# Macaron block: the weighted sums of attention steps 1 to 14 by pairs of heads, in two banks

## The reference

```
x = x + 0.5 * ffn(layernorm(x))
x = x + attn(layernorm(x))
x = x + 0.5 * ffn(layernorm(x))

ffn:  logits = x @ router_w + router_b; top 2 of 8 experts, softmax over the two
      combined = sum_e w_e * silu(x @ expert_w[e].T + expert_b[e])
      y = x + combined @ proj_w.T + proj_b;  rms norm, times norm_w
attn: 16 query heads, 4 key and value heads, head size 128, rope on q and k
      scores = q k^T / sqrt(128), causal;  softmax;  out = P v;  out @ wo.T
```

## Time and profile before

| | |
|---|---|
| median of 3 runs | 827.48 us (825.24 to 830.95) |
| profiled execution, its own time | 827.55 us |
| its span, first to last instruction | 825.8 us |
| TensorE matmul / weight load busy | 792.3 / 697.7 us |
| VectorE / ScalarE / GpSimd busy | 651.9 / 507.4 / 517.2 us |
| share of the chain that ended last | TensorE 82%, VectorE 6%, GpSimd 5%, ScalarE 3% |

### The profile page before, as it was taken

How to read it: one execution, slowest core, us unless ns; L and a number is a source line. 1 busy time by engine, 2 the same in 40 slices (tenths; PEclk the granted TensorE clock), 3 DMA queues, 4 the chain that set the end, 5 groups by cost and what they waited for, 6 DMA issues and landing times.

```text
span 825.8 us, 16045 instructions
## 1 busy us (share of the span) xinstructions
PE 792.3 (96%) x4712; PEld 697.7 (84%) x4712; DVE 651.9 (79%) x1917; ACT 507.4 (61%) x1250; POOL 517.2 (63%) x408
## 2 busy tenths in 40 slices
PE   7899999859999999999999999999999999999996
PEld 4688878658999999999899998999999988788885
DVE  6988996886677686786866868768687799988876
ACT  3565565567667586675765767557576586444543
POOL 4636648693878778787777777877878761112302
PEclk9999999978999999999999999999999999999998
DMA  9245412201132122212312313132131110000001
GB/s 295 86 135 191 148 58 52 52 13 39 27 77 73 41 51 76 51 25 64 102 26 50 88 30 85 27 88 51 31 96 25 39 27 1 1 1 26 2 26 52
DMA packets 28998, 50.09 MB, mean 61 GB/s; under 512 B 3874, under 2 KB 9634, under 8 KB 28962
## 3 DMA queue, kind: packets, MB, share of 16 engines
q1 hardware_dynamic: 28964, 49.67, 21.5%
HBM read 18.72 MB, written 9.96 MB: 35 GB/s over the span
## 4 chain that ended last, share of the span: by engine, by line
PE 82%; DVE 6%; POOL 5%; ACT 3%; issue 2%; DMA 1%; SPq 0%; POOLq 0%; DVEq 0%; ACTq 0%
PE pt L1696 8%; PE pj L1631 5%; PE pj L1633 5%; PE pj L1632 5%; PE o L1710 5%; PE o L1711 4%; PE o L1712 4%; PE sc L1685 4%; PE sc L1684 4%; PE sc L1683 4%; PE pj L1740 4%; PE pj L1742 3%; PE pj L1741 3%; PE sc L973 3%; PE sc L975 3%; PE sc L974 3%
## 5 line engine op out<-in xcount | busy, mean ns | idle before, releaser
L1260 POOL TENSOR_TENSOR at_ql<-at_rot,at_qh 128x512 fp32r<-128x512 f32 x64 | 82.7, 1292 | 103.0 <-ACT at_qh L1485 102.9
L1387 DVE TENSOR_TENSOR at_ptl<-pt,at_pth 128x512 fp32r<-128x512 f32 (+1 forms) x192 | 108.9, 595 | 45.9 <-ACT at_pth L1532 45.6
L1532 ACT ACTIVATE at_pth<-pt 128x512 fp32r<-128x512 f32 (+1 forms) x192 | 94.0, 525 | 81.9 <-PE pt L1696 81.9
L1526 ACT ACTIVATE at_pr<-at_pr,at_low 128x512 f32<-128x512 f32 (+3 forms) x256 | 140.5, 557 | 3.0 <-DVE at_low L1373 2.9
L1272 POOL TENSOR_TENSOR at_rot<-at_rot,gc 128x512 f32<-128x512 f32 x80 | 103.3, 1291 | 6.3
L1382 DVE TENSOR_SCALAR at_pr<-at_pr,at_inv 128x128 f32<-128x128 f32 (+3 forms) x256 | 105.3, 473 | 2.3
L1268 POOL TENSOR_TENSOR at_rot<-ga,cos 128x512 f32<-128x512 f32 x80 | 104.5, 1307 | 2.3 <-POOL at_ql L1260 2.3
L1270 POOL TENSOR_TENSOR gc<-gc,sin 128x512 f32<-128x512 f32 x80 | 103.9, 1299 | 1.0 <-DMA gc<-ga 1.0
L1373 DVE CUSTOM_DVE_ANT_0 at_pr<-sc,at_mask 128x512 f32<-128x512 f32 (+2 forms) x192 | 100.8, 549 | 0.4 <-PE sc L1685 0.3
L1696 PE MATMUL pt<-ident,at_pr 128*128 128x128 f32 x640 | 93.6, 277 | 6.8 <-DVE at_ptl L1387 5.1
L1485 ACT ACTIVATE at_qh<-at_rot 128x512 fp32r<-128x512 f32 x64 | 40.6, 634 | 95.9 <-POOL at_rot L1272 95.9
(11 more groups left out here) (282 smaller groups left out, 2263.6 us busy)
## 6 DMA issues: line engine op xcount, KB each, us to landing
gc<-ga SPq DMA_DIRECT2D x160, 128.0 KB, 2.3
ga<-in_attn_w SPq DMA_DIRECT2D x8, 384.0 KB, 4.8
gb<-attn_split SPq DMA_DIRECT2D x6, 512.0 KB, 4.2
at_wo<-attn_split SPq DMA_DIRECT2D x6, 512.0 KB, 4.3
attn_split<-gb SPq DMA_DIRECT2D x6, 384.0 KB, 2.4
attn_split<-gc SPq DMA_DIRECT2D x6, 384.0 KB, 3.3
x<-in_x SPq DMA_DIRECT2D x4, 512.0 KB, 9.3
e_raw<-in_expert_w SPq DMA_DIRECT2D x8, 256.0 KB, 6.2
```

Of the source, the lines that this page charges most:

```text
L1387: dve.tensor_tensor(ptl[h % 2][:, cols], pt[(NF * h + k) % 2][:, 0:FLEN[k]], pth[h % 2][:, cols].bitcast(F32), ALU.subtract).then_inc(lo_d ...
L1526: act.activation(pr[h % 2][:, cols], pr[h % 2][:, cols], ACT.Exp, bias=low[h % 2][:, i:i + 1], scale=-1.0, accum_out=tot[h % 2][:, i:i + 1 ...
```

## The change

In steps 1 to 14 the heads go by pairs (a, b) = (4s, 4s + 1) and (4s + 2, 4s + 3). The buffers `pth` and `ptl` of the two heads lie side by side in one tensor. The weighted sums of a pair are made together, by halves of the queries: near = query tiles 0 and 1 of both heads, in the bank `pt[0]`, which otherwise takes transposes; far = query tiles 2 and 3 of both, in the bank `o`. A matmul streams the same columns of both heads, as two strips, and so writes 2 x 256 columns, or 2 x 128 where only one of the two query tiles sees the key tile. Near has 2 groups of three matmuls, far 4 groups. One `pair_out_lead` and one `pair_out_rest` take each bank (512 columns, as before). The three transposes of both heads now come ahead of the pair's sums, the scores of the next pair lie between them, and the whole `output(s - 1)` comes after the first pair's transposes. The near bank is a transpose bank, so the first transposes of the next pair wait for the rest of near. In the last step, the three fills of head 60 and the first half of `output(14)` now come first; before, head 60 was transposed in step 14. Step 0 no longer transposes head 4.

```diff
+        PCOL = {kt: FCOL[k] + col for k in range(NF) for kt, col, _ in FILL[k]}
+        NEAR, FAR = ((0, 0), (1, 1)), ((0, 2), (1, 2), (3, 3), (2, 2))
-        pth = [sb(f"pth{n}", [P, TRI], F32R) for n in range(2)]
-        ptl = [sb(f"ptl{n}", [P, TRI], F32R) for n in range(2)]
+        both_h, both_l = sb("pth", [P, 2, TRI], F32R), sb("ptl", [P, 2, TRI], F32R)
+        pth, ptl = ([both[:, n, :] for n in range(2)] for both in (both_h, both_l))
+        def out_pair(far):
+            return (o_ps if far else pt[0])[:].rearrange("p (h q) -> p h q", h=2)
+        def pair_cols(j, far):
+            return slice(2 * j, 2 * j + 2), slice(2 * P * far, 2 * P * (far + 1))
 # VectorE
+            def pair_out_rest(a, j, far):
+                heads, cols = pair_cols(j, far)
+                dve.wait_ge(oh_done, a + far + 1)
+                dve.tensor_tensor(ol[:, heads, cols], out_pair(far), oh[:, heads, cols].bitcast(F32), ALU.subtract).then_inc(ol_done, 1)
+            def pairs(s):
+                for j in range(2):
+                    a = G * s + 2 * j
+                    prob_rest(a, 2 * j, 0)
+                    prob_rest(a, 2 * j, 1)
+                    prob_rest(a, 2 * j, 2)
+                    mask_min(a + 2, 0)
+                    prob_rest(a + 1, 2 * j + 1, 0)
+                    normalise(a + 2, 0)
+                    prob_rest(a + 1, 2 * j + 1, 1)
+                    prob_rest(a + 1, 2 * j + 1, 2)
+                    mask_min(a + 3, 1)
+                    if j == 0:
+                        add_output(s - 1, (0,))
+                        normalise(a + 3, 1)
+                        pair_out_rest(a, j, 0)
+                        add_output(s - 1, (1,))
+                        pair_out_rest(a, j, 1)
+                    else:
+                        pair_out_rest(a, j, 0)
+                        normalise(a + 3, 1)
+                        pair_out_rest(a, j, 1)
+                        value_rest(s + 1)
             def step(s, first, last):
+                if last:
+                    for k in range(NF):
+                        prob_rest(G * s, 0, k)
-                    more1, more2 = not last or h + 1 < G, not last or h + 2 < G
+                    more1, more2 = h + 1 < G, not last or h + 2 < G
 # ScalarE
+            def pair_out_lead(a, j, far):
+                heads, cols = pair_cols(j, far)
+                act.wait_ge(o_ready, a + far + 1)
+                act.activation(oh[:, heads, cols], out_pair(far), ACT.Copy).then_inc(oh_done, 1)
+            def pairs(s, ahead):
+                a, b = G * s, G * s + 1
+                prob_lead(a, 0, 0)
+                prob_lead(a, 0, 1)
+                raw_out(s + 1, 2)
+                prob_lead(a, 0, 2)
+                exps(a + 2, 0, QT[:2])
+                prob_lead(b, 1, 0)
+                exps(a + 2, 0, QT[2:])
+                prob_lead(b, 1, 1)
+                rotated_lead(act, s + 1, 0)
+                value_out(s + 1)
+                prob_lead(b, 1, 2)
+                exps(b + 2, 1)
+                rotated_lead(act, s + 1, 1)
+                pair_out_lead(a, 0, 0)
+                pair_out_lead(a, 0, 1)
+                a, b = G * s + 2, G * s + 3
+                prob_lead(a, 2, 0)
+                prob_lead(a, 2, 1)
+                prob_lead(a, 2, 2)
+                raw_out(s + 1, 3)
+                rotated_lead(act, s + 1, 2)
+                exps(a + 2, 0, QT[:2])
+                prob_lead(b, 3, 0)
+                exps(a + 2, 0, QT[2:])
+                prob_lead(b, 3, 1)
+                prob_lead(b, 3, 2)
+                raw_out(s + 1, 4)
+                if ahead == 2:
+                    raw_out(s + 2, 0)
+                rotated_lead(act, s + 1, 3)
+                exps(b + 2, 1, QT[:2])
+                pair_out_lead(a, 1, 0)
+                exps(b + 2, 1, QT[2:])
+                if ahead == 2:
+                    raw_out(s + 2, 1)
+                pair_out_lead(a, 1, 1)
+                value_lead(s + 1)
+                rotated_lead(act, s + 1, 4)
             def step(s, first, ahead):
+                if not ahead:
+                    for k in range(NF):
+                        prob_lead(G * s, 0, k)
 # TensorE
+            def pair_weigh(a, far):
+                if far:
+                    pe.wait_ge(ol_done, OL0 + a)
+                o = out_pair(far)
+                pe.wait_ge(lo_done, LO0 + NF * a + NF + 2 + far)
+                order = FAR if far else NEAR
+                for n, (kt, i) in enumerate(order):
+                    w = (2 * P if i % 2 == 0 else P)
+                    cols = slice(PCOL[kt] + (i - kt) * P, PCOL[kt] + (i - kt) * P + w)
+                    to, end = o[:, :, 2 * P - w:2 * P], n == len(order) - 1
+                    pe.matmul(to, vh[:, kt, :], both_h[:, :, cols], start=(n == 0), stop=False)
+                    pe.matmul(to, vh[:, kt, :], both_l[:, :, cols], start=False, stop=False)
+                    r = pe.matmul(to, vl[:, kt, :], both_h[:, :, cols], start=False, stop=end)
+                r.then_inc(o_ready, 1)
+            def pairs(s, ahead):
+                a, b = G * s, G * s + 1
+                pe.wait_ge(ol_done, OL0 + a - 1)
+                transpose_p(a, 0, (0,))
+                query(s + 1, 1)
+                transpose_p(a, 0, (1,))
+                value(s + 1)
+                transpose_p(a, 0, (2,))
+                scores(a + 2, s, 2)
+                transpose_p(b, 1, (0, 1))
+                scores(b + 2, s, 3)
+                transpose_p(b, 1, (2,))
+                output(s - 1)
+                pe.wait_ge(vl_done, s + 1)
+                pair_weigh(a, 0)
+                pair_weigh(a, 1)
+                a, b = G * s + 2, G * s + 3
+                pe.wait_ge(ol_done, OL0 + a - 1)
+                transpose_p(a, 2, (0, 1))
+                query(s + 1, 2)
+                transpose_p(a, 2, (2,))
+                scores(a + 2, s + 1, 0)
+                transpose_p(b, 3, (0, 1))
+                query(s + 1, 3)
+                if ahead == 2:
+                    key(s + 2)
+                transpose_p(b, 3, (2,))
+                scores(b + 2, s + 1, 1)
+                if ahead == 2:
+                    query(s + 2, 0)
+                pair_weigh(a, 0)
+                pair_weigh(a, 1)
+                value_T(s + 1, ahead == 2)
             def step(s, first, ahead):
+                if not ahead:
+                    pe.wait_ge(ol_done, OL0 + G * s - 1)
+                    transpose_p(G * s, 0, (0, 1))
+                    output(s - 1, halves=(0,))
+                    transpose_p(G * s, 0, (2,))
-                    more1, more2 = ahead or h + 1 < G, ahead or h + 2 < G
+                    more1, more2 = h + 1 < G, ahead or h + 2 < G
-                        if not first:
-                            output(s - 1, halves=(0, 1) if ahead else (0,))
             with pe.Fori(1, STEPS - 2) as s:
-                step(s, False, 2)
-            step(STEPS - 2, False, 1)
+                pairs(s, 2)
+            pairs(STEPS - 2, 1)
             step(STEPS - 1, False, 0)
```

More of the change, by code:

```diff
@@ L1473, in vector @@
             with dve.Fori(1, STEPS - 1) as s:
-                step(s, False, False)
+                pairs(s)
             step(STEPS - 1, False, True)
```

## The result

The change made the kernel slower by half a per cent: 830.12 us against 826.89 (medians of 15 runs each), ratio 1.0047, interval 1.0031 to 1.0064. The forecast was 823.3, a gain, with a range of 817.8 to 830.0: the time lies just outside it, and the change went the other way. The profiled execution took 829.94 us, with a span of 828.2.

The account below looks back on a forecast made before the run. TensorE, busy throughout the 33.9 us steady step, was taken as the bound, with VectorE's queue deciding the last step. Terms -9.6 + 3.9 + 1.5 = -4.2 us on 827.55 gave 823.3 us, range 817.8 to 830.

Parts of the forecast that it names:

- sums of 14 steps: TensorE's weighted sums: a pair falls from 3.80 to 3.46 us, saving 0.69 a step, 9.6 over 14 steps.
- small waits that the old order had: Steady step before the change: TensorE taken as busy in all 33.9 us, without a gap, so no term.
- value behind normalise: Value projection waits for value_rest, behind a normalise drawn out by GpSimd: 0.3 us a step, 13 times, 3.9 us.
- transposes k = 2 of head b: First pair: they wait for the rest of fill k = 0; between 0 and 0.3 us a step, taken as 0.
- The new waits, one by one: Step of the prediction that lays the engines' orders against each other and costs waits at near bank, transposes and value projection.
- case without a clash: Rival: normalise starts free of GpSimd and value doesn't wait; 819.4 us, down to 817.9; chance 0.27.
- The last step: Step 15: waits of 0.5 and 2.0 us for normalise plus 0.1 at output; loses 1.5 us, bounds 0 and 3.
- head 63's transposes: Last step: TensorE waits 2.0 us for normalise of head 63, VectorE needing 7.95 us against 5.9 on TensorE.
- The tight margins give way: Rival: 0.3 us more a step at the transposes k = 2, 4.2 in all; 827.5 us, no visible change; chance 0.18.
- slower: Rival: near's lead stands behind a late GpSimd, 0.6 us a step, 8.4 in all; 831.7 us; chance 0.08.
- near's lead behind `rotated_lead`: First pair, ScalarE's order: the lead waits for GpSimd's rope; costed at nothing, deciding only from 1.3 us of lateness.
- The dear strips: Rival: two-strip narrow matmuls cost 0.12 us more each, 168 of them, 20 us; 843 us; chance 0.04.

Follow-up runs that it names:

- e6: Changed kernel with the value's split ahead of the far bank's split on ScalarE and VectorE, normalise still before both: 827.98 us, ratio 1.0022 to the kernel before.
- e7: Changed kernel with ScalarE taking the lead of head b's first fill before the second exp of head a + 2: 825.79 us, ratio 0.9995 to the kernel before.
- e5: Changed kernel with the next group's weight load cut in two, query 1, query 2 and value one row earlier: 828.06 us, ratio 1.0017 to the kernel before.
- e3: Changed kernel with pairs in steps 1 to 13 only, step 14 by single heads, step 15 as before: 828.87 us, ratio 1.0033 to the kernel before.
- e9: Changed kernel with e5, e6 and e7 together, pairs kept in step 14: 822.14 us, ratio 0.9941 to the kernel before.
- e11: e10 with ScalarE taking query 1 and value out of their banks right after head 56's first two leads: 816.57 us, ratio 0.9868 to the kernel before.
- e2: Changed kernel with VectorE doing far's rest and value_rest ahead of the normalise of head b + 2: 876.62 us, ratio 1.0617 to the kernel before.
- e10: e8 with query 1 and value placed between head 56's three fills at the start of step 14: 821.57 us, ratio 0.9933 to the kernel before.
- e4: Changed kernel with GpSimd's three rope operations touching 64 of 512 columns from step 2 on: 823.54 us, ratio 0.9960 to the kernel before.
- e1: Changed kernel with the next group's weight load ahead of row 4's two swaps on the queue: 834.71 us, ratio 1.0110 to the kernel before.
- e8: Changed kernel with e5, e6, e7 and e3 together: 818.51 us, ratio 0.9909 to the kernel before; run again, 819.09 us, ratio 0.9901.

## Why the prediction was wrong

It expected a gain of 4.2 us and the kernel lost 3.2. That the change would stay within 1% was its likeliest class and came true, but by losses that it had not seen, not by its sum: -9.6 + 3.9 + 1.5 = -4.2. What the runs give in place of each term, in us for attention:

```
term                                   predicted   measured, and from what
sums of 14 steps                       -9.6        -9.0   2 x (3.80 - 3.48) a step
small waits that the old order had      0          -2.8   33.90 - 0.64 - 33.06 a step
value behind normalise                 +3.9        +4.3   0.33 x 13 (e6: -3.4 net)
transposes k = 2 of head b, output      0          +3.6   0.26 x 14 (e7: -3.7)
query 1 meets the load                  none       +2.4   three long steps (e5: -2.2)
steps 14 and 15                        +1.5        +4.7   the rest of 3.2
sum                                    -4.2        +3.2
```

The last term is a remainder, but it can be read directly too: 49.9 - 45.9 from output(13) to output(15), plus the 0.6 that the sums of step 14 save there, is 4.6.

- **The sums** were right to 6%. A pair is 3.48 us, and writing two strips into a bank costs nothing that the rows show. The Trainium skill's sentence that non-contiguous access to PSUM slows matmuls (SBUF — State Buffer, "Door 1: The DMA port swizzle") isn't borne out for strips of 128 columns: 0.117 us each, against 0.12 for 256 columns without a gap in `output`.
- **The value projection** waited as forecast, by the mechanism forecast: normalise meets GpSimd's last operation and takes 1.92. The case without a clash, to which I gave 0.27, didn't occur; the clash was in every step from 1 to 13. In three of them the wait for the load comes first and covers this one; the table counts it here, and only what is left of the load's below.
- **The transposes k = 2 of head b** are a failed step. The text names the right chain, has it end 0.1 us before TensorE comes, and has bounds of 0 to 0.3; I took 0, "since the chain just fits". It came out at 0.26. A margin of 0.1 out of a layout whose hand-overs are known to about that is no margin, and the middle of the bounds would have been the better value. e7 shows the chain: with one exp less in it the wait is gone.
- **The load of the next group's weights** has no term at all. The step that failed is "The new waits, one by one": it goes through banks and rests, but not through what the moved `query(s + 1, 1)` itself waits for. Before, the load had about 10 us from its issue to the first use; with query 1 second in the step, its issue at 263.11 and the use, due at 268.3, leave 5. e5 shows it.
- **The last step** is the largest miss: 1.5 forecast with a bound of 3, 4.7 measured. I costed step 15 and left out step 14. There neither key nor query 0 of a later step stands between the fills of head b and its sums, so that near waits 1.5 us for a rest of a fill; and that rest stands behind a normalise of 2.75 us. Then output(14) waits 1.3 for far's rest, which stands behind another normalise (1.75 us), where I had 0.1. The rows of TensorE and of VectorE:

```profile
669.75 0.50 PE L1820 MATMUL pt<-at_pth,at_vh 128*128 128x512 f32 x1 [1.54 <-DVE at_ptl L1398]
...
676.14 0.36 PE L1850 MATMUL pj<-at_wo,at_oh 128*128 128x256 f32 x1 [1.33 <-issue]
...
686.55 0.65 PE L1790 MATMUL pt<-ident,at_pr 128*128 128x128 f32 x4 [0.55 <-DVE at_pr L1393]
...
687.48 0.66 PE L1790 MATMUL pt<-ident,at_pr 128*128 128x128 f32 x4 [0.28 <-DVE at_ptl L1398]
...
694.55 1.09 PE L1790 MATMUL pt<-ident,at_pr 128*128 128x128 f32 x8 [1.40 <-DVE at_pr L1393]
```

```profile
666.35 2.75 DVE L1393 TENSOR_SCALAR at_pr<-at_pr,at_inv 128x128 f32<-128x128 f32 x4
```

  The wait at head 63's transposes, which I had at 2.0, is 1.4. e3, e9 and e11 show that this end is a matter of the order of step 14: with single heads there, the end is that of the kernel before (e3).
- **The old order's small waits** went to my favour: I read the steady step as having no gap since TensorE was busy in all of it, but 0.2 us of its 33.9 were slow starts, which count as busy. Most of it stands in one place: the scores at 228.70 take 1.97 us to the next work's start, those of the other heads of that step 1.83 to 1.85.
- **The rivals.** "The tight margins give way" (0.18) was the nearest by mechanism, which held at one of its two places. By the number, 831.7 of the "slower" case (0.08) was the nearest, but that is chance: near's lead behind `rotated_lead` cost nothing, and in the steady steps no sum and no first transposes waited for the near bank. The dear strips didn't occur.

Two causes stay unresolved. The start of the program differs by up to 4.5 us between traces of the same first part. The granted clock has a share in it: in the two with the latest first output (e2 and e10) it is 0.97 over the first 50 us, where the others have 1.00; the rest is open. And of the 4.7 us at the end the trace names some 4.3 as waits (1.5, 1.3, 0.8, 1.4 and 0.3, less the 1.1 that were there before); how they hang together was shown only for the whole, not for each.

## What to carry to other kernels

When a piece of work moves in a hand-written order, list what that piece itself waits for, its loads too, and the price of the cover in the steps where the loop body is cut short, not in the full one alone. A gain of 0.64 us in each step of 33.9 was eaten by four waits that came to 2.4 to 4.7 us each over attention. Three of them went by moving a line or two or by cutting a load in two; the fourth by keeping the old order in step 14. A wait can cost more than its length: behind some of them the matmuls ran at a lower clock. An instruction that shares a resource with another engine has no one duration: read it at each place where it stands, with what the other engine runs in that moment.

## What the runs showed of the hardware

- VectorE's normalise (four tensor_scalar instructions, SBUF to SBUF) can be held by several GpSimd operations in a row, 1.27 to 4.03 us for the same work (e2), while GpSimd's own operations in that moment stay at 1.29 to 1.38 us against 1.30. The Trainium skill (SBUF — State Buffer, "SBUF: two separate sides") says that a shared port pair is locked for a whole instruction, for certain kinds of VectorE instruction, and the other engine fully blocks; by that rule, the trace agrees. That VectorE then comes last again and again against short gaps the page doesn't say, and no run here shows whether a longer gap would do.
- In e4 a wait of 1.9 us for the load is followed by slow matmuls (0.42 apart instead of 0.23); the granted clock of the stretch is 0.68, so that part of it ran at the lower level, 1.2 and not 2.4 GHz:

```profile
267.00:269.70 2.70, 0.85 (x8) 0.62 (x6) 2.42 (x5) 2.09 (x4) 1.00 (x1) 1.00 0.77 211
269.72:275.00 5.28, 5.28 (x19) 4.32 (x20) 0.80 (x2) 1.09 (x2) 1.16 (x4) 0.68 0.01 2
275.00:279.00 4.00, 4.00 (x28) 3.71 (x28) 2.79 (x11) 2.75 (x9) 0.00 (x0) 1.00 0.29 66
```

  The same follows waits of TensorE of 1.68 us in e1, 1.94 in e9, 2.61 in e10 and 2.67 in e2. It doesn't follow waits of 1.95 in e1, 1.92 in e6 and 2.08 in e3 and e8, nor any in the changed kernel's steps 1 to 15 (1.54 and less), where the clock is 1.00. So the length of the one wait doesn't decide it; what does, these runs leave open. Where it happened it cost about 1.5 us.
